# Splitting the next context early, moving late logits to a bank of their own, and one silu table load for all experts

## The chip, the cores and the metric

The kernel runs on one core of a Trainium2 chip. The metric is the device time of one execution in microseconds (us), the median over several runs. Its engines work in parallel and wait for each other by semaphores: TensorE (PE) multiplies, ScalarE (ACT) applies functions and copies, VectorE (DVE) does elementwise work and reductions, GpSimd (POOL) and SyncE (SP) mainly issue DMA transfers. SBUF is the memory that the engines share, PSUM the one into which TensorE writes, in banks of 512 float32 per partition.

## The reference

Four sequences of 1024 tokens, width 1024, float32. Three layers, each with a layernorm ahead and a residual behind:

```
x = x + attention(layernorm(x))                     # 16 heads, causal, rotary
x = x + mix(layernorm(x), ctx)                      # below
x = x + experts(layernorm(x))                       # 64 experts, 8 for each token

def mix(t, ctx):                                    # ctx [B, 1024, 512], D = 128
    query, key = ctx @ Wq.T + bq, ctx @ Wk.T + bk   # [B, 1024, 128]
    attention = softmax(query @ key.T)              # [B, 1024, 1024]
    return t @ attention.T                          # features are mixed, [B, 1024, 1024]

def experts(t):
    logits = t @ gate.T                             # 64 per token
    ...                                             # top 8, some experts mapped onto others
    y = (silu(t @ Wgate[e]) * (t @ Wup[e])) @ Wdown[e]
```

## The kernel before

Every float32 product is made from three: both operands are split into a high part (a rounded copy, made by ACT) and a low part (operand less high part, made by DVE), and `split_product` issues high x high, high x low and low x high into one PSUM bank. So each operand passes ACT, then DVE, before TensorE may use it.

The program has four stages: self attention, mixing (`mix_features`), routing, and the experts (`experts`). Each engine has its own list of instructions, written out by hand; the order within a list is fixed, and an instruction that waits holds up all behind it on that engine. TensorE's order is the schedule.

**Mixing** goes over the four batches b. For a batch the context (512 x 1024, four quarters of 256 columns, one DMA each into one of the two slots of `stage`) is split into `at_hi` and `at_lo`, which later hold the attention matrix. `project_ctx(b, n)` makes queries and keys of half n of the columns (L912) with 24 matmuls; ACT and DVE split these into `qk` (`split_qk`, `rest_of_qk`, L1055 and L1152). Then follow eight rows of blocks i: `energies` into `ps_b` (L926), `maxima` on DVE (L1161), `exps` on ACT (L1071), `invert` on DVE, `normalise_rows` on ACT (L1076), `turn_attention` (eight transposes, L939), and a split into `at_hi` and `at_lo` (L1080, L1170). While ACT and DVE do that, TensorE gets halves of the attention output's projection for token blocks 0 and 1 as filling work: `PARTS` lists them and `FILL` says after which energies each comes (L739). The projection's input is loaded into `stage`, too, and split into `split[:, 0:2]` (`split_attn_out`, L1087, `rest_of_attn_out`, L1175).

Then comes the loop over the batch's eight token blocks: `project`, layernorm (`normalise(2, g)`, L1198), `turn(2, g)` (transposes), `split_ln2` and `rest_of_ln2` (L1092, L1209), `mix` (48 matmuls into `ps_b`), `add_mix`, a second layernorm (`normalise(3, g)`), its store, `turn(3, g)`, a copy to `x3_t` (L1097), and `route_logits` (L996), the 64 logits of the experts, one block behind the mix. The last block's transposes, its logits and the two halves of the next context's projection come after the last mix, in turns. The next context can only be split after it, as `at_hi` and `at_lo` are in use until then (`split_ctx` waits for `xm_ok`, L1052).

**Experts.** A loop over 64 experts (`for_experts`, L1574): `super_block` handles 512 rows of an expert, an inner loop `tail_block` 128 more each, if there are more. At the top of each round every engine reads from SBUF how many tail blocks lie before this expert and the next (`tails_before`, L1571). Weights stream through a ring of three slots `raw_w`; ACT copies the high parts (`split`, L1883), DVE makes the low ones (`rest_of`, L2062), and TensorE's first layer of an expert waits for them. After the first two chunks and the last block's result, ACT runs one tiny silu on `warm`:

```
                finish_last(e + t0)
                act.activation(warm[:, :], warm[:, :], ACT.Silu)
                split(2)
```

ACT's functions need a table in the engine; the compiler places the ACT_TABLE_LOAD instructions, they are in no line of the kernel.

## Time and profile before

| | us |
|---|---|
| median of the three runs shown | 7848.82 (7845.66 to 7859.39) |
| the profiled execution | 7843.7 |
| its span in the profile | 7841.7 |
| TensorE busy | 7236.3 (92%) |
| DVE, ACT, POOL busy | 4006.6, 3616.8, 1745.8 |

The span is what the profile covers, from the first to the last instruction; a little lies around it. The profile's rows name an instruction by the line of the kernel, the engine, and the tile written and read. A line of a helper stands for all its callers: L908 to L910 are all split products of the mixing, L1702 to L1704 those of the experts, told apart by their tiles (`ps_r` and `xw_hi`: context projection; `ps_b` and `xattn_qk`: energies; `ps_a`: attention output's projection; `ps_b` and `at_hi`: mix). What stands in brackets behind an instruction is the idle time of its engine before it and what ended it. The granted clock is the share of full speed (2.4 GHz) at which TensorE was let run.

### The profile page before, as it was taken

Reading aid. Unit: us, or ns where it says so; the run is one execution under the profiler, and the core shown is the slowest. Engines: PE = TensorE matmul, PEld = TensorE weight load, DVE = VectorE, ACT = ScalarE, POOL = GpSimd, SP = SyncE. Lnnn points to the kernel's source line nnn. Section 1 sums busy time; section 2 is a strip of 40 time slices with the busy share of each in tenths; the row PEclk is TensorE's granted clock in tenths of the full one; section 3 lists DMA queues with packets and bytes.
Section 4 is the critical chain, followed back from the end, with each engine's and each line's share of the span. In section 5 each row is a group of like instructions: output and inputs, shape, how many; then the busy total and the mean of one; then the engine's idle time right before and its main releaser. Section 6 shows DMA issues by size and latency. Waiting matters only on the chain.

```text
span 7841.7 us, 126591 instructions
## 1 busy us (share of the span) xinstructions
PE 7236.3 (92%) x39855; PEld 6135.6 (78%) x39856; DVE 4006.6 (51%) x8015; ACT 3616.8 (46%) x6744; POOL 1745.8 (22%) x1646
## 2 busy tenths in 40 slices
PE   8997997997996889985699999999999999999999
PEld 7886886886885777874588888888888888888887
DVE  6666666666665433345444444444444444444444
ACT  5665664665665221120244444444444444444444
POOL 1111111111110000000233333333333333333333
PEclk9998998998998999997799999999999999999999
DMA  1101111111111222121356555565555565555655
GB/s 58 34 25 47 30 33 43 34 28 41 33 33 64 67 68 84 65 71 40 113 161 169 159 157 159 156 174 158 158 158 158 160 180 158 158 160 158 161 158 147
DMA packets 290687, 826.52 MB, mean 105 GB/s; under 512 B 36000, under 2 KB 111776, under 8 KB 290336
## 3 DMA queue, kind: packets, MB, share of 16 engines
q0 software_dynamic: 98928, 365.58, 20.2%
q1 hardware_dynamic: 191408, 456.61, 17.5%
q8 instruction: 178, 2.92, 0.2%
q14 instruction: 173, 1.42, 0.1%
HBM read 615.37 MB, written 206.70 MB: 105 GB/s over the span
## 4 chain that ended last, share of the span: by engine, by line
PE 48%; issue 2%; DVE 1%; ACT 1%; ACTq 1%; POOL 0%; DMA 0%; DVEq 0%; POOLq 0%
PE ps_gu L1702 10%; PE ps_gu L1704 10%; PE ps_gu L1703 10%; PE ps_y L1702 4%; PE ps_y L1704 4%; PE ps_y L1703 4%; PE ps_xe L1722 3%; PE ps_xe L1731 1%; PE ps_l L1711 1%; ACTq L1572 1%; DVE gu_lo L2062 1%; ACT gu_hi L1883 1%; PE ps_h L1814 0%; DVE logits L1976 0%; ACT xtail_hi L1855 0%
## 5 line engine op out<-in xcount | busy, mean ns | idle before, releaser
L1702 PE MATMUL ps_gu<-xs_hi,gu_hi 128*128 128x512 f32 x3072 | 1223.7, 398 | 45.7 <-DVE gu_lo L2062 45.7
L1704 PE MATMUL ps_gu<-xs_hi,gu_lo 128*128 128x512 f32 x3072 | 1205.4, 392 | 0.0
L1703 PE MATMUL ps_gu<-xs_lo,gu_hi 128*128 128x512 f32 x3072 | 1200.6, 391 | 0.0
L347 PE MATMUL ps_qkv<-w_hi,xt_hi 128*128 128x384 f32 x1920 | 709.0, 369 | 52.0 <-DVE v L637 51.9
L1702 PEld LDWEIGHTS ps_gu<-xs_hi,gu_hi 128*128 128x128 f32 x3072 | 577.9, 188 | 189.7 <-DVE gu_lo L2062 73.6
L1681 POOL TENSOR_TENSOR dn_lo<-raw_w,dn_hi 128x512 fp32r<-128x512 f32 x384 | 485.1, 1300 | 907.1 <-ACT dn_hi L1883 907.1
L1704 PEld LDWEIGHTS ps_gu<-xs_hi,gu_lo 128*128 128x128 f32 x3072 | 577.4, 188 | 129.4
L1703 PEld LDWEIGHTS ps_gu<-xs_lo,gu_hi 128*128 128x128 f32 x3072 | 578.2, 188 | 120.6
L707 DVE TENSOR_TENSOR pt_lo<-ps_t,pt_hi 128x512 fp32r<-128x512 f32 (+3 forms) x768 | 424.8, 553 | 451.9 <-ACT pt_hi L556 439.0
L347 PE MATMUL ps_qkv<-w_hi,xt_lo 128*128 128x384 f32 x1920 | 651.5, 339 | 0.0
L347 PE MATMUL ps_qkv<-w_lo,xt_hi 128*128 128x384 f32 x1920 | 649.4, 338 | 0.0
L1702 PE MATMUL ps_y<-dn_hi,hs_hi 128*128 128x512 f32 x1536 | 628.6, 409 | 0.0
L1895 ACT ACTIVATE hs_hi<-act_s 128x512 fp32r<-128x512 f32 x192 | 121.3, 632 | 1081.7 <-DVE act_s L2067 1081.7
L2062 DVE TENSOR_TENSOR gu_lo<-raw_w,gu_hi 128x512 fp32r<-128x512 f32 x768 | 482.3, 686 | 252.5 <-ACT gu_hi L1883 251.0
L1704 PE MATMUL ps_y<-dn_hi,hs_lo 128*128 128x512 f32 x1536 | 606.8, 395 | 0.0
L1703 PE MATMUL ps_y<-dn_lo,hs_hi 128*128 128x512 f32 x1536 | 606.2, 395 | 0.0
L2067 DVE TENSOR_TENSOR act_s<-ps_gu,act_s 128x512 f32<-128x512 f32 x192 | 132.7, 691 | 898.7 <-PE ps_gu L1704 898.7
L2022 DVE TENSOR_TENSOR xs_lo<-ps_xe,xs_hi 128x512 fp32r<-128x512 f32 x520 | 334.4, 685 | 478.5 <-ACT xs_hi L1847 478.5
L556 ACT ACTIVATE pt_hi<-ps_t 128x512 fp32r<-128x512 f32 (+3 forms) x768 | 375.1, 488 | 343.3 <-PE ps_t L433 328.6
L1659 POOL DMA_INDIRECT out<-y_sup,scatter_s x192 | 303.1, 1579 | 1012.1 <-ACT y_sup L1905 983.0
L1905 ACT ACTIVATE y_sup<-ps_y,w_now 128x512 f32<-128x512 f32 x384 | 264.4, 689 | 438.4 <-PE ps_y L1704 421.5
L502 ACT ACTIVATE probs<-probs,inv_sum 128x128 f32<-128x128 f32 (+7 forms) x512 | 397.6, 777 | 120.1 <-DVE inv_sum L665 114.0
(296 smaller groups left out, 16403.3 us busy)
## 6 DMA issues: line engine op xcount, KB each, us to landing
raw_w<-w_gu SPq DMA_DIRECT2D x384, 512.0 KB, 4.0
raw_w<-w_down SPq DMA_DIRECT2D x192, 512.0 KB, 6.8
w_raw<-wqkv SPq DMA_DIRECT2D x260, 192.0 KB, 2.6
out<-residual SPq DMA_DIRECT2D x36, 512.0 KB, 2.6
probs<-x SPq DMA_DIRECT2D x32, 512.0 KB, 3.8
attn_out<-out_t POOLq DMA_DIRECT2D x128, 128.0 KB, 2.2
residual<-x SPq DMA_DIRECT2D x32, 512.0 KB, 4.9
stage<-attn_out SPq DMA_DIRECT2D x32, 512.0 KB, 5.7
```

Of the source, the lines that this page charges most:

```text
L347: mm = pe.matmul(out, xs[:, k, a], ws[:, k, :], start=(n == 0), stop=(n == 3 * HB - 1))
L502: act.activation(probs[g][:, i, 0:keys], probs[g][:, i, 0:keys], ACT.Copy, scale=inv_sum[:, n:n + 1]).then_inc(norm_ok, 1)
L556: act.activation(pt_hi[:, s % 2, off:], ps_t[:, (TB - 1 + at) % 2, off:], ACT.Copy).then_inc(tile_hi_ok, 1)
L707: dve.tensor_tensor(pt_lo[:, s % 2, off:], ps_t[:, (TB - 1 + at) % 2, off:], raw(pt_hi[:, s % 2, off:]), ALU.subtract).then_inc(tile_lo_ok, 1)
L1659: pool.indirect_dma_start(out, bass.IndirectOffsetOnAxis(ap=scatter_s[:, i:i + 1], axis=0), y_sup[:, i % 2, :], None, compute_op=ALU.add). ...
L1681: pool.tensor_tensor(dn_lo[:, f, a], raw_w[:, f, a], raw(dn_hi[:, f, a]), ALU.subtract).then_inc(dn_lo_ok, 1)
L1702: pe.matmul(out, a_hi, w_hi, start=first, stop=False)
L1703: pe.matmul(out, a_hi, w_lo, start=False, stop=False)
L1704: return pe.matmul(out, a_lo, w_hi, start=False, stop=last)
L1905: act.activation(y_sup[:, i % 2, a], ps_y[:, a], ACT.Copy, scale=w_now[:, i:i + 1]).then_inc(ys_ok, 1)
L2022: dve.tensor_tensor(xs_lo[:, ks, a], ps_x1[:, c * BANK:(c + 1) * BANK].rearrange("p (k c) -> p k c", c=P), raw(xs_hi[:, ks, a]), ALU.subtr ...
L2062: dve.tensor_tensor(gu_lo[:, c // 2, b], raw_w[:, c % RING, a], raw(gu_hi[:, c // 2, b]), ALU.subtract).then_inc(lo_ok, 1)
```

## The change

In the mixing:
- The four quarters of the next context go to four places: the first to `split[:, 0:2]` (free once the batch's attention outputs are projected), the second to the second half of `qk` (free after the batch's energies), the third and fourth to `at_hi` and `at_lo` as before. `project_ctx` therefore works on quarters, 256 columns a matmul.
- SyncE loads the first two quarters two blocks earlier, the third and fourth within the last block. ACT and DVE split the first two before the last mix, the others after it.
- TensorE's order at the end of a batch: turn(2, last), mix(last, 0), turn(3, last - 1), mix(last, 1), project_ctx 0, logits of block 6 (into `ps_a`, first bank), project_ctx 1, turn(3, last). The logits of block 7 go into the second bank of `ps_a`, after the next batch's first energies and the first filling projection.
- The filling projections come at i = 0, 1, 2, 3, 5, 6, 7 instead of 1, 2, 3, 4, 6, 7 and after the loop; the attention outputs are split one or two instructions earlier, and the normalised block 0 goes into the space of `x3_t`, in DVE's round 6.

In the experts: the tiny silu moves from each round to once before the loop, and DVE's low parts of the first two chunks (`first_weights`) come before the round's reads of the block counts.

```diff
@@ -736,7 +736,7 @@
     PARTS = [(i, c, part) for i in range(2) for c in range(HALVES) for part in range(2)]
-    FILL = {1: PARTS[0], 2: PARTS[1], 3: PARTS[2], 4: PARTS[3], 6: PARTS[4], 7: PARTS[5]}
+    FILL = dict(zip((0, 1, 2, 3, 5, 6, 7), PARTS))
@@ -752,9 +752,14 @@
-ctx_hi_sb, ctx_lo_sb = at_hi[:, 0:CB, :], at_lo[:, 0:CB, :]
...
+first_x2 = x3_t[:, :, :].rearrange("p k c -> p (k c)")
+ctx_sb = [[split[:, n, :].rearrange("p (a c n) -> p a c n", a=2, n=QW) for n in range(2)],
+          [qk[:, 2 * n:2 * n + 2, BANK:].rearrange("p a (c n) -> p a c n", n=QW) for n in range(2)],
+          [t[:, 0:CB, 0:QW].rearrange("p (a c) n -> p a c n", a=2) for t in (at_hi, at_lo)],
+          [t[:, 0:CB, QW:2 * QW].rearrange("p (a c) n -> p a c n", a=2) for t in (at_hi, at_lo)]]
@@ -873,21 +877,22 @@
                 load_attn(g + 2)
-            elif b + 1 < B:
-                sp.wait_ge(ot_lo, START + g + 1)
-                load_ctx(b + 1, i + 2 - TB)
+            if i in (TB - 4, TB - 3) and b + 1 < B:
+                sp.wait_ge(ot_lo, START + g + 3)
+                load_ctx(b + 1, i + 4 - TB)
+            if i == TB - 1 and b + 1 < B:
+                rest_of_ctx(b + 1)
...
-            rest_of_ctx(b + 1)
+            first_attn(b + 1)
+        store_x3(b * TB + TB - 1)
+        if b + 1 < B:
...
-            first_attn(b + 1)
-        else:
-            store_x3(N - 1)
@@ -915,12 +920,13 @@
             pe.wait_ge(proj_lo, START + (b * 2 + n) * 2)
-            pe.wait_ge(r_read, START + max(0, b * TB - 1))
+            pe.wait_ge(r_read, START + max(0, b * TB - 2))
...
-            half_n = slice(n * BANK, (n + 1) * BANK)
-            for c in range(CB):
-                mm = split_product(ps_r[:, w, :], xw_hi[:, c, w * D:(w + 1) * D], xw_lo[:, c, w * D:(w + 1) * D],
-                                   ctx_hi_sb[:, c, half_n], ctx_lo_sb[:, c, half_n], c == 0, c == CB - 1)
+            for q in range(2):
+                hi, lo = ctx_sb[2 * n + q]
+                for c in range(CB):
+                    mm = split_product(ps_r[:, w, q * QW:(q + 1) * QW], xw_hi[:, c, w * D:(w + 1) * D], xw_lo[:, c, w * D:(w + 1) * D],
+                                       hi[:, c // 2, c % 2, :], lo[:, c // 2, c % 2, :], c == 0, c == CB - 1)
@@ -955,7 +961,8 @@
             pe.wait_ge(x1_ok, START + g)
-            pe.wait_ge(r_read, START + g // TB * TB)
+        pe.wait_ge(r_read, START + g // TB * TB - (g % TB == 0 and c == 0 and g > 0))
@@ -976,8 +983,9 @@
                 pe.wait_ge(t3_read, START + g)
+        src = first_x2 if which == 2 and i == 0 else work[:, which - 2, :]
...
-            mm = pe.transpose(ps_t2[:, k * P:(k + 1) * P], work[:, which - 2, k * P:(k + 1) * P], ident[:, :])
+            mm = pe.transpose(ps_t2[:, k * P:(k + 1) * P], src[:, k * P:(k + 1) * P], ident[:, :])
@@ -1013,29 +1022,33 @@
                 turn_attention(b, i - 1)
-        project(g + 1, 1, (0,))
+            elif b:
+                route_logits(g - 1, ps_a[:, BANK:])
         turn_attention(b, TB - 1)
...
         project(g + 1, 1, (1,))
-        for i in range(TB):
-            if i >= 1:
-                if i + 1 < TB:
-                    project(g + i + 1, 0, (0, 1))
-                turn(2, g + i)
-                if i + 1 < TB:
-                    project(g + i + 1, 1, (0, 1))
-                turn(3, g + i - 1)
+        mix(g, 0)
+        mix(g, 1)
+        for i in range(1, TB - 1):
+            project(g + i + 1, 0, (0, 1))
+            turn(2, g + i)
+            project(g + i + 1, 1, (0, 1))
+            turn(3, g + i - 1)
             mix(g + i, 0)
-            if i >= 1:
-                route_logits(g + i - 1, ps_r[:, 0, :])
+            route_logits(g + i - 1, ps_r[:, 0, :])
             mix(g + i, 1)
         last = g + TB - 1
+        turn(2, last)
+        mix(last, 0)
+        turn(3, last - 1)
+        mix(last, 1)
         if b + 1 < B:
             project_ctx(b + 1, 0)
-        turn(3, last)
+        route_logits(last - 1, ps_a[:, 0:BANK])
         if b + 1 < B:
             project_ctx(b + 1, 1)
-        route_logits(last, ps_a)
+        turn(3, last)
+    route_logits(N - 1, ps_a[:, BANK:])
@@ -1049,8 +1062,13 @@
+            act.wait_ge(wo_ok, START + b * TB)
+        elif q == 1:
+            act.wait_ge(e_ok, START + b * TB)
+        else:
...
-        act.activation(ctx_hi_sb[:, :, q * QW:(q + 1) * QW], raw_ctx(q), ACT.Copy).then_inc(ctx_hi, 1)
+        act.activation(ctx_sb[q][0], raw_ctx(q), ACT.Copy).then_inc(ctx_hi, 1)
@@ -1106,18 +1124,19 @@
         g = b * TB
+        split_attn_out(g)
         for i in range(TB):
+            if i == 4:
+                split_attn_out(g + 1)
             exps(b, i)
...
                 split_attention(b, i - 2)
-            if i == 5:
-                split_attn_out(g + 1)
+            elif i == 0 and b:
+                copy_logits(g - 1, ps_a[:, BANK:])
             normalise_rows(b, i)
-            if i == 0:
-                split_attn_out(g)
         split_attention(b, TB - 2)
         split_attention(b, TB - 1)
-        for i in range(TB):
+        for i in range(TB - 1):
             split_ln2(g + i)
@@ -1125,16 +1144,20 @@
         last = g + TB - 1
+        split_ln2(last)
         if b + 1 < B:
...
             split_ctx(b + 1, 1)
-            split_qk(b + 1, 0)
-        copy_ln3(last)
+        copy_ln3(last - 1)
         if b + 1 < B:
...
             split_ctx(b + 1, 3)
+            split_qk(b + 1, 0)
+        copy_logits(last - 1, ps_a[:, 0:BANK])
+        if b + 1 < B:
             split_qk(b + 1, 1)
-        copy_logits(last, ps_a)
+        copy_ln3(last)
+    copy_logits(N - 1, ps_a[:, BANK:])
@@ -1146,8 +1169,8 @@
         dve.wait_ge(ctx_hi, START + b * QUARTERS + q + 1)
-        a = slice(q * QW, (q + 1) * QW)
-        dve.tensor_tensor(ctx_lo_sb[:, :, a], raw_ctx(q), raw(ctx_hi_sb[:, :, a]), ALU.subtract).then_inc(ctx_lo, 1)
+        hi, lo = ctx_sb[q]
+        dve.tensor_tensor(lo, raw_ctx(q), raw(hi), ALU.subtract).then_inc(ctx_lo, 1)
@@ -1195,7 +1221,8 @@
             dve.wait_ge(x3_out, START + g * 16)
-        dve.tensor_scalar(work[:, s, :], res[:, g % 2, :], mean_var[:, s, 0:1], rstd[:, s:s + 1],
+        dst = first_x2 if which == 2 and i == 0 else work[:, s, :]
+        dve.tensor_scalar(dst, res[:, g % 2, :], mean_var[:, s, 0:1], rstd[:, s:s + 1],
@@ -1220,19 +1247,21 @@
         g = b * TB
+        rest_of_attn_out(g)
         for i in range(TB):
+            if i == 4:
+                add_projection(g)
             maxima(b, i)
+            if i == 4:
+                rest_of_attn_out(g + 1)
             if i >= 2:
...
             invert(b, i)
-            if i == 0:
-                rest_of_attn_out(g)
             if i == 5:
-                add_projection(g)
-                rest_of_attn_out(g + 1)
                 find_moments(2, g)
+            if i == 6:
+                normalise(2, g)
         rest_of_attention(b, TB - 2)
-        normalise(2, g)
         rest_of_attention(b, TB - 1)
@@ -1240,6 +1269,9 @@
                 normalise(2, g + i + 1)
+            elif b + 1 < B:
+                rest_of_ctx(b + 1, 0)
+                rest_of_ctx(b + 1, 1)
@@ -1248,14 +1280,13 @@
         if b + 1 < B:
-            rest_of_ctx(b + 1, 0)
-            rest_of_ctx(b + 1, 1)
+            rest_of_ctx(b + 1, 2)
+            rest_of_ctx(b + 1, 3)
         find_moments(3, last)
+        if b + 1 < B:
+            rest_of_qk(b + 1, 0)
         normalise(3, last)
         if b + 1 < B:
-            rest_of_qk(b + 1, 0)
-            rest_of_ctx(b + 1, 2)
-            rest_of_ctx(b + 1, 3)
             rest_of_qk(b + 1, 1)
@@ -1571,9 +1602,11 @@
-def for_experts(eng, super_block, tail_block):
+def for_experts(eng, super_block, tail_block, first=None):
...
+        if first:
+            first(e)
@@ -1864,6 +1897,7 @@
     act.wait_ge(set_up, START + 13)
+    act.activation(warm[:, :], warm[:, :], ACT.Silu)
@@ -1907,7 +1941,6 @@
         finish_last(e + t0)
-        act.activation(warm[:, :], warm[:, :], ACT.Silu)
@@ -2053,14 +2086,18 @@
+    def rest_of(e, c):
+        for q in range(2):
+            dve.wait_ge(hi_ok, START + e * 2 * CHUNKS + 2 * c + q + 1)
+            a = slice(q * BANK, (q + 1) * BANK)
+            b = slice(c % 2 * HALF + q * BANK, c % 2 * HALF + (q + 1) * BANK)
+            dve.tensor_tensor(gu_lo[:, c // 2, b], raw_w[:, c % RING, a], raw(gu_hi[:, c // 2, b]), ALU.subtract).then_inc(lo_ok, 1)
+    def first_weights(e):
+        rest_of(e, 0)
+        rest_of(e, 1)
...
-        def rest_of(c):
-            for q in range(2):
-                dve.wait_ge(hi_ok, START + e * 2 * CHUNKS + 2 * c + q + 1)
-                a = slice(q * BANK, (q + 1) * BANK)
-                b = slice(c % 2 * HALF + q * BANK, c % 2 * HALF + (q + 1) * BANK)
-                dve.tensor_tensor(gu_lo[:, c // 2, b], raw_w[:, c % RING, a], raw(gu_hi[:, c // 2, b]), ALU.subtract).then_inc(lo_ok, 1)
@@ -2144,7 +2179,7 @@
-    for_experts(dve, super_block, tail_block)
+    for_experts(dve, super_block, tail_block, first_weights)
```

The diff leaves out: the same bank and wait changes at four more places, the reshaped view of `stage`, and calls of `rest_of` that got the expert's number as an argument. Indentation is cut by eight.

## Rows read from the trace of the kernel before

**Rows 1.** Windows: us, busy time of each engine, granted clock, DMA.
```profile
3110.77:3166.60 55.83, 45.47 (x218) 35.84 (x218) 26.84 (x32) 29.39 (x36) 0.74 (x2) 0.94 0.04 10
3114.80:3123.40 8.60, 6.83 (x18) 4.90 (x19) 2.69 (x4) 4.58 (x7) 0.00 (x0) 0.60 0.21 61
3807.00:7829.00 4022.00, 3984.58 (x21562) 3311.64 (x21563) 1822.93 (x3315) 1806.78 (x3180) 1308.64 (x1021) 1.00 0.59 161
```

**Rows 2.** Timeline of TensorE, end of batch 1: start, duration, instruction, wait.
```profile
3065.44 1.03 PE L980 MATMUL ps_t<-ident,work 128*128 128x128 f32 x8
3071.46 1.71 PE L980 MATMUL ps_t<-ident,work 128*128 128x128 f32 x8 [4.99 <-DVE split L1209]
3090.62 0.50 PE L908 MATMUL ps_r<-at_hi,xw_hi 128*128 128x512 f32 x1 [3.71 <-DVE at_lo L1150]
...
3096.31 1.03 PE L980 MATMUL ps_t<-ident,work 128*128 128x128 f32 x8
3101.79 0.50 PE L908 MATMUL ps_r<-at_hi,xw_hi 128*128 128x512 f32 x1 [4.45 <-DVE at_lo L1150]
...
3109.04 1.89 PE L1000 MATMUL ps_a<-gate_sb,x_t 128*128 128x64 f32 x16
3110.77 0.50 PE L908 MATMUL ps_b<-xattn_qk 128*128 128x512 f32 x1
```

**Rows 3.** TensorE's waits in the energies of batch 2 (total, times, longest).
```profile
PE ps_a L908 <- DVE split L1175: 4.5, 2, 3.0
PE ps_b L908 <- ACT work L1071: 3.1, 2, 2.6
PE ps_t L980 <- DVE work L1198: 1.8, 1, 1.8
PE ps_t L950 <- ACT work L1076: 0.9, 1, 0.9
```

**Rows 4.** Groups by line on DVE and ACT, 3064.4 to 3166.6 us.
```profile
L1161 DVE TENSOR_REDUCE mix_small<-ps_b 128x1 f32<-128x1024 f32 x8 | 9.7, 1214 | 7.6 <-PE ps_b L910 7.6
...
L1071 ACT ACTIVATE work<-ps_b,mix_small 128x1024 f32<-128x1024 f32 x8 | 8.9, 1116 | 14.9 <-DVE mix_small L1161 14.9
```

**Rows 5.** Timeline of TensorE, matmuls of 256 columns in a tail block.
```profile
4817.24 0.28 PE L1702 MATMUL ps_gu<-gu_hi,xtail_hi 128*128 128x256 f32 x1
4817.36 0.28 PE L1703 MATMUL ps_gu<-gu_lo,xtail_hi 128*128 128x256 f32 x1
```

**Rows 6.** All table loads of the run, groups by line on ACT.
```profile
L1883 ACT ACT_TABLE_LOAD x64 | 82.1, 1283 | 58.4 <-issue 58.4
L1910 ACT ACT_TABLE_LOAD x64 | 82.1, 1283 | 1.2
L472 ACT ACT_TABLE_LOAD x1 | 1.3, 1283 | 5.9 <-PEq L69 5.9
```

**Rows 7.** Timeline around the start of an expert, all engines.
```profile
4885.40 1.28 ACT L1883 ACT_TABLE_LOAD   x1 [0.98 <-issue]
...
4886.69 2.19 ACT L1883 ACTIVATE gu_hi<-raw_w 128x512 fp32r<-128x512 f32 x4
...
4887.10 0.39 PE L1704 MATMUL ps_y<-dn_hi,hs_lo 128*128 128x512 f32 x1
4887.36 1.90 DVE L2062 TENSOR_TENSOR gu_lo<-raw_w,gu_hi 128x512 fp32r<-128x512 f32 x3 [2.11 <-ACT gu_hi L1883]
...
4888.10 0.50 PE L1702 MATMUL ps_gu<-xs_hi,gu_hi 128*128 128x512 f32 x1 [0.62 <-DVE gu_lo L2062]
...
4888.44 0.40 PE L1703 MATMUL ps_gu<-xs_lo,gu_hi 128*128 128x512 f32 x1
```

**Rows 8.** TensorE's waits in the experts.
```profile
PE ps_gu L1702 <- DVE gu_lo L2062: 45.7, 64, 8.3
```

**Rows 9.** Reads of the block counts before one expert, by queue.
```profile
L1572 PEldq SEQ_ASSERT  x2: 18/18/18, 4884.7 to 4885.4; - x2
L1572 DVEq SEQ_ASSERT  x2: 23/28/33, 4885.8 to 4887.0; - x2
```

20 lines of the change are left out of this document (10 added, 10 removed).

## The prediction, made before the changed kernel was run

> **What bounds the kernel now.** The table of stretches comes first. In the experts (3807 to 7829 us) TensorE is busy 3984.6 of 4022 us at a granted clock of 1.00, so only TensorE's own gaps can be won there. In the mixing, the loop over eight token blocks has none; the gaps sit in the stretch around the next context and in the 56 us stage of energies, where the granted clock also falls to 0.94 [rows 1]. The timeline of TensorE then shows the end of a batch: from the turn of the last block (3065.44) to the next batch's first energies (3110.77) are 45.33 us, with waits of 4.99, 3.71 and 4.45 [rows 2]. The list of waits gives 10.3 us for the energies [rows 3]. For the experts the list gives one reason, gu_lo: 45.7 us in 64 waits, one of 8.3, so (45.7 - 8.3) / 63 = 0.59 each [rows 8]. Ends of matmuls are modelled, 0.39 us after the start, while the next one can start 0.24 later (24 of them in 5.69 us, 3090.62 to 3096.31) [rows 2, 7], so each wait costs 0.16 us more than its row says, and the first matmul after it delays the next by 0.34 instead of 0.24 (4888.10 to 4888.44), 0.10 more [rows 7].
>
> **Context and logits (mixing), between batches 1 and 2.** The change loads the first two quarters of the next context two blocks earlier and splits them, into other buffers, while DVE waits for the last mix. Their four instructions stay; they move off the path.
> - Removed: the wait before the first half's projection, 3.71 + 0.16 = 3.87 us. mix(last, 1) now ends and project_ctx(0) starts.
> - Removed: the wait before the second half, from 3096.31 + 0.79 (eight transposes) to 3101.79 = 4.69 us [rows 2]. Its splits can start at the end of the last mix, and take add_mix, two ACT and two DVE instructions, about 3.7 us in all for tiles of this size at 1.1 to 1.2 us with DVE and ACT overlapping [rows 4]; over them lie project_ctx(0) (5.7 us) and the moved logits (1.7). The covers are worth 3.7 us if they fail.
> - Removed with it: the low clock behind that wait. The second projection took 3101.79 to 3109.04 = 7.25 us, the first 3090.62 to 3096.31 = 5.69: 1.56 us.
> - Moved: the last block's logits, 3109.04 to 3110.77 = 1.73 us, to behind the next first energies [rows 2]. It is paid again below.
> - Added: one wait before the energies, since turn(3) (0.79 us) no longer covers the split of the second projection on ACT and DVE. Before, the energies started 1.73 us after the projection, as soon as the logits let them [rows 2], and the chain itself needs about 1.75; without the logits 0.96 us stay open.
> - Added: each half is now 48 matmuls of 256 columns instead of 24 of 512. Starts of such ones are 0.12 us apart (48 in 5.7 us to be expected) against 0.24 [rows 5]: +0.45 us a batch, with 0.1 for the first half's tiles being split just before the second half may start.
> - The wait of 4.99 stays: DVE still normalises block 6 before it splits block 7's transposes.
> Sum: 3.87 + 4.69 + 1.56 + 1.73 - 0.96 - 0.55 = 10.3 us.
>
> The 256 columns are the place where a page would speak against the change. The row: 256-column matmuls, each with weights of its own, start 0.12 us apart [rows 5], so loads are hidden. The Trainium skill, "TensorE: Matmul & The Clock Gate", section "LDWEIGHTS (loading the stationary operand)", gives 128 columns / 1.2 = 107 ns a load, and its section on packing says that loads overlap only other row groups; an estimate from it is 0.21 us for each pair and 9 us more a batch, some 37 in all. The trace disagrees.
>
> **The energies.** I walk the new order with 1.45 us for six matmuls, 2.8 for a half projection, 0.79 for transposes, and 1.21 and 1.12 us for maxima and exps, normalising about like exps [rows 4]. From the first energies (0): ACT copies block 7's transposes and splits the attention output, DVE its rest, so the projection starts at 2.85 instead of 1.45 (wait 1.4); logits to 7.35; energies 1 at 7.35, 3 at 17.45, 4 at 22.5. Block 4 now has no projection: turning 3 waits 1.3, and energies 5, behind add_projection, maxima and a longer ACT queue, 1.65. Energies 7 wait 1.1 for DVE's moments. The last projection stands before turn 6, so turn 7 waits 4.2 for maxima, exps and normalising of block 7, and the turn of the normalised block 1.4 for rest_of_attention(6). That is 11.05 us; the same six waits of before are 10.3 + 6 x 0.16 = 11.3 [rows 3]. So: 55.83 - 11.3 + 11.05 + 1.73 (logits) = 57.3. Before, 8.6 us of this stage ran at 0.60 [rows 1], which cost about 0.4 x 6.8 busy us = 2.7. Nothing says where a dip falls in the new order: none gives 54.6, one as before 57.3. I take half, 56.0: no gain, -1.4 to +1.4 a batch.
>
> Batch 0 has no logits there and its first attention tile is long split when the energies start: about 3.0 us less, 0.4 back for the narrower matmuls. At the very end the logits of block 30 move behind the last mix, into the wait for the last normalised block: 1.7 us. SyncE's new waits hold up no store: in DVE's order each stands before the add_mix whose result that store needs.
>
> Mixing: 3 x (10.3 - 0.1) + 2.6 + 1.7 = 35 us.
>
> **The experts.** Every expert begins with an ACT_TABLE_LOAD of 1.28 us in front of a plain copy, and has another for the silu warm-up; the whole of attention and mixing, whose exps also stand in loops, has one [rows 6]. The chain at the start of an expert: table load 4885.40, first split at 4886.69 (0.64 us), its rest on DVE 4887.36, TensorE 4888.10, while the last matmul had started at 4887.10 and could have been followed at 4887.34 [rows 7]. Two edits act here. With silu loaded once before the loop, state at entry and at the loop's end agree, and both loads should vanish: split at 4885.40, done 4886.04. DVE's reads of the block counts end only at 4887.0 [rows 9]; alone they would still make its rest late by 0.5 us. The new order puts the first splits ahead of them: rest from 4886.07 to 4886.76, 0.57 us before TensorE needs it. TensorE's own reads end at 4885.4, under queued matmuls [rows 9]. What comes later on DVE (w_now, gather indices) is about 1.1 us later against TensorE; its users are the gathers for the next turns, which stand whole layers behind. Gain per expert 0.59 + 0.16 + 0.10 = 0.86 us, the first about the same by the reads; 64 x 0.86 = 55 us. If a load stays at the top, the gain is 0.
>
> The trace shows that copies run behind the silu load without a load of their own, but one stands ahead of the first copy of each round [rows 6, 7]. The Trainium skill, "ScalarE: Activation LUTs", section "Table sets: the hidden batching unit", says that copy is in every set; by that rule no load in the loop is needed, and the one at the top is only the compiler's. The trace agrees as to the copies behind silu. The page's other figure, 2.66 us a switch with its drain, no row shows: the next activation starts 0.01 us behind the 1.28.
>
> **Rivals.**
> 1. The load at the loop's top stays. For it: it is there 64 times. Against: one load in all earlier loops [rows 6]. The experts gain nothing: 7759 + 55 = 7814 us.
> 2. The second half of the context comes late after all (its transfers start behind the last block's store and x load) and a wait of 4.6 us comes back three times: 7759 + 14 = 7773. Against it: they can start about 12 us before the last mix ends.
> 3. Narrow matmuls cost their shown 0.28 us each [rows 5]: 4 x 96 x (0.28 - 0.12) = 61: 7820. Against it: the starts in the same rows. The page's rule on weight loads would act here too, with less.
> 4. Slower: TensorE without gaps gets a lower clock in the experts. Seen there: 1.00 [rows 1]. At the energies' 0.94 it would cost 4022 x (1/0.94 - 1) = 257: 8016 us. It decides from a clock of 0.974 down. Against it: gaps lowered the clock so far, not their absence.
>
> **Numbers.** 35 + 55 = 90 us off. The profiled execution took 7843.7 (span 7841.7, 2.0 around it), 5.1 below the median of the runs shown, 7848.8; I take 90 from the median: 7759 us; the new profile's span should be about 7752. Chances: forecast 0.80, rival 1 0.09, rival 2 0.07, rival 3 0.02, rival 4 0.01, nothing at all (two of them together) 0.01. The forecast's own range, with dips (4 x 1.4), gaps (0.1 us an expert either way) and the spread of the medians, is 7742 to 7776; with rival 2 to 7788. A change of 0.2% (16 us) is about what the measurement can tell: faster 0.97, same 0.02, slower 0.01.
>
> **What would show it.** In the changed kernel: one or two table loads on ACT in all; no TensorE wait for gu_lo from the second expert on, a stage of some 3967 us at clock 1.00; no wait before ps_r's projections or one under 0.3 us; first energies 35 us behind the turn of block 7; waits of 1.4 and 4.2 us in the energies, which should last 54.6 to 57.3 us. Wrong: loads left in the loop, a wait for the context, or the energies beyond 58 us.

## The result, and the profile after

The changed kernel takes 7749.9 us (median of 4 runs, 7742.4 to 7753.8) where the kernel before takes 7850.9 (4 runs beside them, 7845.7 to 7859.4): a ratio of 0.9868, 95% interval 0.9856 to 0.9881, or 101 us less. The forecast was 7759 in a range of 7742 to 7776, or to 7788 with rival 2. The runs of the two kernels don't overlap. The profiled execution has a span of 7747.5 us (7841.7 before).

First the windows of the changed kernel: energies of batch 1, its eight blocks up to the turn of the last one, the stretch from there to the next energies, and the experts. Columns: stretch, us, then busy time (instructions) of TensorE, its weight loads, VectorE, ACT and POOL, granted clock, DMA share, GB/s.

```profile
2833.44:2887.47 54.03, 47.09 (x232) 38.59 (x233) 26.82 (x32) 29.67 (x37) 0.74 (x2) 0.94 0.04 10
2887.47:3052.52 165.05, 165.05 (x817) 137.79 (x816) 60.06 (x77) 19.46 (x24) 9.59 (x26) 1.00 0.24 80
3052.52:3086.81 34.29, 28.70 (x186) 25.79 (x184) 15.51 (x19) 9.58 (x12) 1.48 (x4) 0.95 0.48 154
3764.22:7734.68 3970.46, 3970.38 (x21562) 3316.61 (x21563) 1834.51 (x3315) 1630.92 (x2991) 1298.71 (x1021) 1.00 0.60 163
```

They answer to [rows 1]. In the experts TensorE is now busy in all but 0.1 us of its stretch. Taken from the starts of the same instructions in both timelines, in us:

| stretch | before | after | won | forecast |
|---|---|---|---|---|
| energies of batch 0 | 55.8 | 51.4 | 4.4 | 2.6 with the first context |
| energies of batches 1, 2, 3 | 55.8, 55.9, 55.9 | 54.0, 53.2, 53.2 | 7.1 | -0.3 |
| turn of the last block to the next energies, three times | 45.4, 45.3, 45.3 | 34.8, 34.3, 34.3 | 32.6 | 30.9 |
| turn of the last block to the last logits copied, batch 3 | 32.5 | 31.3 | 1.2 | 1.7 |
| first expert matmul to the last one | 4022.3 | 3970.5 | 51.8 | 54 |
| last logits copied to first expert matmul | 176.4 | 175.3 | 1.1 | 0.9 |
| from the start to the first context matmul | 2561.0 | 2564.8 | -3.9 | 0 |

The rows add up to 94.3, the difference of the two spans (94.2). The last one is code that the change doesn't touch; the experiments show that it varies by itself. So does the mixing stage, by up to 10.9 us between profiled executions of the same mixing code (below), so the gains of the mixing in this table are those of one execution each.

The end of batch 0 on TensorE (start, duration, instruction, wait ahead of it and who ended it):

```profile
2798.61 1.04 PE L988 MATMUL ps_t<-ident,work 128*128 128x128 f32 x8
2804.54 0.79 PE L913 MATMUL ps_b<-at_hi,split 128*128 128x512 f32 x1 [4.89 <-DVE split L1236]
...
2806.41 0.63 PE L914 MATMUL ps_b<-at_lo,split 128*128 128x512 f32 x1
2806.84 0.63 PE L915 MATMUL ps_b<-at_hi,split 128*128 128x512 f32 x1
...
2818.66 0.28 PE L913 MATMUL ps_r<-split,xw_hi 128*128 128x256 f32 x1
...
2824.26 1.89 PE L1009 MATMUL ps_a<-gate_sb,x_t 128*128 128x64 f32 x16
2826.03 0.36 PE L913 MATMUL ps_r<-at_hi,xw_hi 128*128 128x256 f32 x1
...
2831.71 1.03 PE L988 MATMUL ps_t<-ident,work 128*128 128x128 f32 x8
2833.44 0.50 PE L913 MATMUL ps_b<-xattn_qk 128*128 128x512 f32 x1 [0.69 <-DVE xattn_qk L1179]
```

Against [rows 2]: both waits before ps_r's projections are gone and both projections run at full clock (5.60 and 5.68 us); one wait of 0.69 is new; the wait of 4.9 for the last block's split has stayed. Behind it the mix matmuls start 0.43 us apart, not 0.23: the low clock is part of that wait's price.

TensorE's waits in the experts and all table loads of the run, against [rows 8] and [rows 6]:

```profile
PE ps_gu L1735 <- DVE gu_lo L2094: 7.3, 1, 7.3
```

```profile
L472 ACT ACT_TABLE_LOAD x1 | 1.3, 1283 | 5.9 <-PEq L69 5.9
L1900 ACT ACT_TABLE_LOAD x1 | 1.3, 1283 | 29.5 <-PEq L69 29.5
```

And the start of one expert, against [rows 7]: no table load, the rest of chunk 0 on VectorE 0.7 us behind ACT, and TensorE goes from ps_y to ps_gu in 0.23 us.

```profile
4829.27 2.20 ACT L1917 ACTIVATE gu_hi<-raw_w 128x512 fp32r<-128x512 f32 x4 [1.00 <-issue]
...
4829.94 2.49 DVE L2094 TENSOR_TENSOR gu_lo<-raw_w,gu_hi 128x512 fp32r<-128x512 f32 x4 [0.83 <-ACT gu_hi L1917]
...
4830.95 0.40 PE L1737 MATMUL ps_y<-dn_hi,hs_lo 128*128 128x512 f32 x1
4831.18 0.39 PE L1735 MATMUL ps_gu<-xs_hi,gu_hi 128*128 128x512 f32 x1
```

The waits of TensorE in the energies of batch 1, against [rows 3]. Each row is a total, the number of waits and the longest; the walk had 1.4 where the first projection's 1.0 stands, 1.3 for turn 3 and 4.2 for turn 7 where ps_r's 4.3 stands for both, 1.65 for energies 5 (the row of 1.3) and 1.1 for energies 7, 1.4 for the turn of the normalised block (ps_t). The 0.7 is the new wait ahead of the first energies. The rows leave out the 0.16 us behind each wait.

```profile
PE ps_r L956 <- ACT work L1094: 4.3, 2, 3.4
PE ps_b L913 <- ACT work L1089: 1.3, 1, 1.3
PE ps_a L913 <- DVE split L1198: 1.0, 1, 1.0
PE ps_b L913 <- DVE xattn_qk L1179: 0.7, 1, 0.7
PE ps_t L988 <- DVE at_lo L1193: 0.3, 1, 0.3
```

### The profile page after: what moved, and what is told of

Same layout as the page of the kernel before. It is cut to its first block, busy times and chain, and to the rows that moved or that the text cites. A ratio compares the mean times of both kernels' runs of the same rounds, so it can differ in the third digit from the quotient of the medians.

```text
span 7747.5 us, 126837 instructions
## 1 busy us (share of the span) xinstructions
PE 7219.9 (93%) x40047; PEld 6153.2 (79%) x40048; DVE 4017.3 (52%) x8015; ACT 3437.1 (44%) x6554; POOL 1735.5 (22%) x1646
## 4 chain that ended last, share of the span: by engine, by line
PE 51%; DVE 0%; DMA 0%; POOL 0%; issue 0%; ACT 0%; DVEq 0%; POOLq 0%; ACTq 0%
PE ps_gu L1737 10%; PE ps_gu L1735 10%; PE ps_gu L1736 10%; PE ps_y L1735 5%; PE ps_y L1737 5%; PE ps_y L1736 5%; PE ps_xe L1755 3%; PE ps_xe L1764 1%; PE ps_l L1744 1%; PE ps_h L1847 0%; DVE logits L2009 0%; DMA out<-y_sup,scatter_s 0%; DMA x_rows<-rows,gather_s 0%; DVE xs_lo L2055 0%; DVE at_hi L2002 0%
## 5 line engine op out<-in xcount | busy, mean ns | idle before, releaser
L347 PE MATMUL ps_qkv<-w_hi,xt_hi 128*128 128x384 f32 x1920 | 709.5, 370 | 51.9 <-DVE v L637 51.8
L1917 ACT ACTIVATE gu_hi<-raw_w 128x512 fp32r<-128x512 f32 x768 | 427.2, 620 | 230.4 <-DMA raw_w<-w_gu 170.8
```

Source lines behind the costliest of these rows:

```text
L347: mm = pe.matmul(out, xs[:, k, a], ws[:, k, :], start=(n == 0), stop=(n == 3 * HB - 1))
L1917: act.activation(dst[:, a], raw_w[:, c % RING, a], ACT.Copy).then_inc(hi_ok, 1)
```

## The experiments

"Mixing stage" below is the time from the first context matmul to the start of the last logits: 1065.45 us before, 1020.17 after. Ratios are to the kernel before on the same chip.

**The two parts, each alone.** The one kernel has the mixing of before and the experts of after, the other the reverse; no line besides.

> The mixing of before with the experts of after (silu loaded once ahead of the loop, VectorE's first_weights ahead of its reads). Theory: the two parts of the change add up, so this one is worth what the stage of the experts showed in the trace of after, 53 us (52 to 55): a ratio of 0.9933, first expert matmul to last ps_y start 3970.5 us (4022.3 before), boundary of the mixing 45.3 us as before. Rival: part of those 53 us comes from the mixing's new state (a higher clock or other DMA traffic carried over), then the stage stays over 3980 us here.

> The mixing of after with the experts of before. Theory: the mixing stage alone gives its 45 us (mixing stage 1024.1 us against 1069.4; ratio 0.9943), and the experts stay at 4022 us with 64 table loads ahead of the first copy and 64 for the silu. Rival: the stage before it also moved by 3.9 us between the two traces although its code is the same; if the change causes that, this kernel shows it too, with its first context matmul at 2564.8 and not at 2561.0.

Experts alone: 7796.1 us, ratio 0.9925 (0.9908 to 0.9941), stage of the experts 3969.9. Mixing alone: 7796.3 us, ratio 0.9929 (0.9912 to 0.9945), mixing stage 1022.9, experts 4023.2 with 64 and 64 table loads. (The 1024.1 and 1069.4 of its expectation are counted to the copy of the last logits, 3.9 us later.) The parts add up: 4022.3 - 3969.9 = 52.4 and 1065.5 - 1022.9 = 42.5 make 94.9, against 51.8 + 45.3 = 97.1 for both together. (By the medians the parts are 56.0 and 55.9 us, 112 against 101 for both; the intervals of the ratios, about 13 us either way for each part, allow for that.) The rival of a carried-over state falls: the stage of the experts is 3969.9 us with the mixing of before. The first context matmul started at 2561.1 with the changed mixing and at 2568.3 with the old one; over all kernels here it lay between 2558.8 and 2569.1, with the same code ahead of it. So the 3.9 us in the table are variation of that stage, not the change.

One thing was not expected: with the mixing's code as before, the kernel with the new experts needed 1073.1 us for that stage, 7.7 more than before. The granted clock accounts for it. Take the busy time of TensorE in windows of 1 us, times the share of the clock that it lacks there, and add this up over the mixing stage (us, one profiled execution each; the last rows belong to experiments below):

| kernel | mixing | stage | low clock | stage less low clock |
|---|---|---|---|---|
| before | before | 1065.5 | 25.4 | 1040.0 |
| e_silu_once_only | before | 1066.8 | 26.6 | 1040.2 |
| e_experts_only | before | 1073.1 | 33.7 | 1039.4 |
| e_dve_first_only | before | 1076.3 | 36.9 | 1039.4 |
| after | after | 1020.2 | 19.4 | 1000.8 |
| m_mixing_only | after | 1022.9 | 21.8 | 1001.1 |
| m_late_loads | later loads | 1020.9 | 20.1 | 1000.8 |
| m_logits_early | earlier logits | 1024.0 | 24.1 | 999.9 |
| m_fill_late | later filling | 1019.5 | 14.9 | 1004.6 |
| m_keep_warm | dummies | 1020.9 | 17.3 | 1003.7 |
| v_rest_first | VectorE's order | 1011.0 | 20.1 | 990.9 |
| v_split_first | more order | 1001.3 | 14.5 | 986.7 |
| v_order_all | more order | 991.9 | 10.4 | 981.5 |

Four executions of one mixing code differ by 10.9 us in the stage and by 0.8 once the low clock is taken out. Of the 45.3 us that the change won in the mixing, 39.2 are in the last column and 6.0 in the low clock, and the second part could have come out some us either way. The split is not exact between different orders: low clock that a later wait covers costs nothing and is taken out all the same (see the dummy matmuls). One such stretch in e_experts_only (a wait on TensorE, then a window: stretch, us, busy, clock, DMA share, GB/s): it begins 1.3 us behind the end of a wait of 2.96, where the profiled execution of before has the same wait (3148.21) and keeps its clock.

```profile
3156.49 0.50 PE L908 MATMUL ps_a<-wo_hi,split 128*128 128x512 f32 x1 [2.96 <-DVE split L1175]
```

```profile
3157.00:3162.00 5.00, 5.00 (x20) 0.66 0.00 0
```

**The experts' two edits, each alone.** Both on the kernel before.

```diff
+            act.activation(warm[:, :], warm[:, :], ACT.Silu)     # e_silu_once_only: ahead of the loop
...
-                act.activation(warm[:, :], warm[:, :], ACT.Silu)
```

```diff
-            for_experts(dve, super_block, tail_block)                # e_dve_first_only
+            for_experts(dve, super_block, tail_block, first_weights)
```

> Before, with one edit: the silu warm-up stands once ahead of the loop; VectorE still reads its block counts ahead of the rest of chunk 0. Theory: the table loads vanish from the loop and ACT's first split is done at about 4886.04 on before's clock, but VectorE is busy with its reads to 4887.0, so TensorE starts at about 4887.75 in place of 4888.10: 0.35 us an expert, 22 us in all, ratio 0.9972, and a wait for gu_lo of some 0.25 us stays in every round. Rival: the reads aren't in the way and all 53 us come here (0.9933).

> Before, with the other edit alone: VectorE's rest of chunks 0 and 1 ahead of its reads of the block counts; the silu warm-up stays in each round, with both table loads. Theory: ACT's table load and first split end at 4887.33 on before's clock and VectorE's reads at 4887.0, so TensorE is held by ACT: 0 to 2 us in all, ratio 1.000. Rival: the reads are what holds TensorE, and this edit gives 20 us or more by itself (0.9975 or less).

Silu once: 7837.9 us (10 runs), ratio 0.9983 (0.9974 to 0.9993), experts 4009.9: 12.4 us won. VectorE's order alone: 7852.9 us (10 runs), ratio 1.000 (0.999 to 1.0009), experts 4022.0. The edits are a pair: 12.4 and 0.3 us in the stage apart, 52.4 together, since two things end the same wait. (By the medians Silu once wins 14 us and VectorE's order nothing.) Silu once, waits in the experts and the start of an expert:

```profile
PE ps_gu L1702 <- DVE gu_lo L2062: 31.6, 63, 8.3
```

```profile
4886.16 0.68 DVE L2022 TENSOR_TENSOR xs_lo<-ps_xe,xs_hi 128x512 fp32r<-128x512 f32 x1
...
4887.01 2.19 ACT L1884 ACTIVATE gu_hi<-raw_w 128x512 fp32r<-128x512 f32 x4 [1.00 <-issue]
...
4888.69 0.39 PE L1704 MATMUL ps_y<-dn_hi,hs_lo 128*128 128x512 f32 x1
4888.81 2.50 DVE L2062 TENSOR_TENSOR gu_lo<-raw_w,gu_hi 128x512 fp32r<-128x512 f32 x4 [1.97 <-ACT gu_hi L1884]
...
4889.55 0.50 PE L1702 MATMUL ps_gu<-xs_hi,gu_hi 128*128 128x512 f32 x1 [0.47 <-DVE gu_lo L2062]
```

No table load stands ahead of ACT's split, and its first part is long done when VectorE starts at 4888.81, 1.97 us behind the end of its last instruction (4886.84). The row names ACT, but ACT isn't what held it: with the reads behind the rest, the same idle time is 0.83 in after's expert shown above. What fills the gap are the reads of the block counts on VectorE's queue (count, shortest, median and longest in ns, start of the first and the last):

```profile
L1572 DVEq TENSOR_LOAD <-starts x2: 316/556/796, 4886.9 to 4887.6; - x2
L1572 DVEq SEQ_ASSERT  x2: 23/28/33, 4887.4 to 4888.6; - x2
```

They begin as VectorE's last instruction ends, and the last part of them stands 0.2 us before the next one. So two register reads on VectorE cost 1.97 us here from instruction to instruction. The 22 us expected were worked out with the end of the reads' own rows, 1.75 us [rows 7, 9], and were 0.15 us an expert too many (0.19 measured for 0.35); the waits that stay are (31.6 - 8.3) / 62 = 0.38 us for 0.25.

In the other kernel the load is still there and ends the wait, as in [rows 7]:

```profile
4896.07 1.28 ACT L1885 ACT_TABLE_LOAD   x1 [0.98 <-issue]
4897.37 2.19 ACT L1885 ACTIVATE gu_hi<-raw_w 128x512 fp32r<-128x512 f32 x4
...
4898.78 0.50 PE L1704 MATMUL ps_gu<-xs_hi,gu_hi 128*128 128x512 f32 x1 [0.61 <-DVE gu_lo L2063]
```

**Are the early loads of the context needed?** After, with the two loads at the place of before.

```diff
-                    if i in (TB - 4, TB - 3) and b + 1 < B:
-                        sp.wait_ge(ot_lo, START + g + 3)
-                        load_ctx(b + 1, i + 4 - TB)
+                    if i in (TB - 2, TB - 1) and b + 1 < B:
+                        sp.wait_ge(ot_lo, START + g + 1)
+                        load_ctx(b + 1, i + 2 - TB)
```

> After, with the loads of the next context's first two quarters issued two blocks later, as before did. Theory: the early loads are not needed; the first quarter is split behind the last block's transposes and the second one arrives before project_ctx(0) is due, so the boundary stays at 34.3 us and the time at after's (ratio to before 0.987). Rival: the second quarter comes behind the store and the x load of its block and late; a wait before project_ctx(0) of 2 to 4 us comes back three times, 6 to 12 us in all, boundary 36.5 to 38.5.

7748.6 us, ratio 0.9865 (0.9849 to 0.9882), mixing stage 1020.9: no difference. ACT now waits for the second quarter's transfer, but in the cover of the last mix:

```profile
3068.70 1.06 ACT L1071 ACTIVATE xattn_qk<-stage 128x1024 fp32r<-128x1024 f32 x1 [8.24 <-DMA stage<-ctx_t]
```

The projection starts at 3076.89. With 1.2 us for VectorE's part, about 6 us of slack are left. The rival's wait did not come, and it is not the time of the loads that wins at this place. What is left is the buffers of their own, which let the splits run beside the last mix; the splits without them weren't tried, since they would overwrite what the last mix reads.

**Narrow matmuls.** After, with each mix matmul as two of 256 columns.

```diff
-                n = slice(c * BANK, (c + 1) * BANK)
-                for k in range(TB):
...
+                for q in range(2):
+                    n = slice(c * BANK + q * QW, c * BANK + (q + 1) * QW)
+                    for k in range(TB):
```

> After, with every mix matmul of 512 columns issued as two of 256 with a weight load each: 32 blocks x 48 = 1536 become 3072. Theory: weight loads are hidden under matmuls of 256 columns, starts are 0.12 us apart and two of them take what one of 512 takes (0.237): 1536 x 0.003 = 5 us and the change of tiles nothing; ratio to before 0.987 to 0.989. Rival (page rule on weight loads): the load of 128 columns isn't covered, each pair costs 0.19 to 0.21 us more, 290 to 320 us in all, ratio about 1.025.

7760.1 us, ratio 0.9881 (0.9864 to 0.9897), mixing stage 1040.8, 20.6 us more (11.5 and 14.7 against the medians of m_late_loads and m_fill_late on the same chip; in the profiled execution 9 us of it are missing again in stages that the edit doesn't touch). The weight loads are hidden; the rival's 290 to 320 us are not there.

```profile
2911.32 0.28 PE L913 MATMUL ps_b<-at_hi,split 128*128 128x256 f32 x1
2911.44 0.28 PE L914 MATMUL ps_b<-at_lo,split 128*128 128x256 f32 x1
2911.56 0.28 PE L915 MATMUL ps_b<-at_hi,split 128*128 128x256 f32 x1
```

The theory's 5 us were too few: it took 0.237 us for the wide matmul, from the context projection, where those of the mix start 0.227 apart (2795.65 to 2798.37 in 12 steps, in the timeline of after). Two narrow ones take 0.24, so a pair costs 0.013 more, 20 us for 1536.

**Where the last filling stands.** After, with its seventh half projection ahead of turn 7 and not of turn 6.

```diff
-    FILL = dict(zip((0, 1, 2, 3, 5, 6, 7), PARTS))
+    FILL = dict(zip((0, 1, 2, 3, 5, 6), PARTS))
...
+                project(g + 1, 1, (0,))
                 turn_attention(b, TB - 1)
```

> After, with its seventh filling half projection (2.8 us on TensorE) moved from ahead of turn 6 to ahead of turn 7. Theory: turn 7 is bound by the chain of maxima, exps, reciprocal and normalising of block 7, which doesn't move, so the wait of 3.4 ahead of turn 7 shrinks by 2.8 to about 0.6, 2.8 us less stand ahead of turn 6, and the stage of energies stays at 53.2 to 54.0 us. Rival A: the filling is only worth its place where it is, and the stage grows by 1 to 3 us. Rival B: turn 6 comes earlier and with it the rest of its chain, and the stage shrinks by 1 us or more.

7745.4 us, ratio 0.9864 (0.9847 to 0.988), energies of batches 1 to 3 53.6, 52.7, 52.7: 0.5 us less each. The theory missed that turn 6 would have to wait: the 3.4 became 1.8 ahead of turn 6 and 1.4 ahead of turn 7, not 0.6. Turn 7 itself runs at full clock, and the turn of the normalised block waits 1.2 in place of 0.3. But that turn starts 49.90 us behind batch 1's first energies, 49.86 in after. So the theory's main point holds: a chain over ACT and VectorE sets the end of this stage, and the fillings only cover it.

**Block 7's logits ahead of the energies again.**

```diff
                 turn(3, last)
-            route_logits(N - 1, ps_a[:, BANK:])
+                route_logits(last, ps_a[:, BANK:])
```

(and the copy on ACT behind copy_ln3(last); the calls behind energies 0 go.)

> After, with block 7's logits ahead of the next batch's first energies again, behind turn(3, 7). Theory (the prediction's terms: 1.73 us moved, 0.96 of it paid back as a wait): the logits need the copy of block 7's transposes, which ACT makes behind the split of the second projection, so the first energies start 2.3 us later than in after (boundary 36.6 us), and the energies lose the 1.73 us of logits but keep the wait for the attention output they covered: the stage falls by 1.5; 0.8 us a batch more in all, 2 to 3 us in the kernel. Rival: the logits behind the energies were cover that is missed more than that, or the low clock of the energies' start comes back, 2 us a batch or more.  The other rival: their place is worth nothing.

7749.5 us, ratio 0.9869 (0.9852 to 0.9885), mixing stage 1024.0: 3.8 us more in the profile, nothing in the median. From one batch's mix to the next energies it is 1.7, 2.8 and 2.2 us longer, the energies are 0.9, 1.5 and 0.1 shorter; in batches 1 and 3 a stretch of low clock is back just behind the first energies (2830 to 2835 us and 3339 to 3343 us). The table above puts all of it down to the low clock: 24.1 us for 19.4, while the rest of the stage is 0.9 us shorter. So the 0.8 us a batch that the theory expected do not show apart from it. Whether the logits' place brings the low clock back isn't shown either, since after's own mixing code varied by 2.4 us of it between two executions (m_mixing_only).

**Dummy matmuls in the longest wait.**

```diff
+                pe.wait_ge(eexp_ok, START + (b + 1) * TB)
+                for k in range(12):
+                    pe.matmul(ps_b[:, 0:BANK], wo_hi[:, 0, 0:P], wo_hi[:, 0, 0:BANK], start=True, stop=True)
                 turn_attention(b, TB - 1)
```

> After, with twelve matmuls of 512 columns that nothing uses (2.8 us) put into the wait of 3.4 us ahead of turn 7, in a bank that is free then. Theory: the stretch of low clock that follows this wait comes from the idle time in it; TensorE's clock stays at 1.00 there, the eight transposes of turn 7 take 1.03 us in place of 1.97, and the stage of energies shrinks by 1.0 to 1.5 us (2.7 in batch 0), 5 to 7 us in the kernel. Rival A: the low clock comes from what ran before (the waits of the whole stage) or from elsewhere and stays: gain 0. Rival B: the stage only gets the dip at another place.

7742.8 us, ratio 0.986 (0.9843 to 0.9876). Turn 7 in after, and here:

```profile
2881.04 1.97 PE L956 MATMUL ps_r<-ident,work 128*128 128x128 f32 x8 [3.41 <-ACT work L1094]
```

```profile
2870.55 2.99 PE L1029 MATMUL ps_b<-wo_hi 128*128 128x512 f32 x12
2873.72 1.09 PE L956 MATMUL ps_r<-ident,work 128*128 128x128 f32 x8 [0.17 <-ACT work L1097]
```

The next instruction, the turn of the normalised block, in after and here:

```profile
2883.30 1.54 PE L988 MATMUL ps_t<-ident,x_t 128*128 128x128 f32 x8 [0.29 <-DVE at_lo L1193]
```

```profile
2875.97 1.07 PE L988 MATMUL ps_t<-ident,x_t 128*128 128x128 f32 x8 [1.17 <-DVE at_lo L1196]
```

The low clock is gone from turn 7, in all four batches, and in m_fill_late too, so it hung on the long wait there. But turn 7's transposes got 0.88 us faster and the wait behind them 0.88 longer: the turn of the normalised block needs VectorE's rest of block 6 and comes when that is done. Most of what the low clock cost at turn 7 was covered. The energies change by -1.7, -0.8, +0.4 and -0.5 us; in batch 2 a stretch of low clock has come at energies 5 (the window below). The other stretches grow by 0.7, 0.7, 0.2 and 1.8, with longer low clock behind the wait of 4.9, and the mixing stage is 1020.9 us, no shorter.

```profile
3106.00:3110.00 4.00, 2.92 (x7) 0.60 0.00 0
```

Rival B holds in part: some of the low clock moved, and some of it had cost nothing. The profiled execution is 8 us shorter than after's, but 6 of them lie ahead of the first context matmul, in the stage that varies.

**Three versions that go further.** The first takes the wait of 4.9 apart: VectorE's moments and normalising of block 6 stand in front of the split that TensorE waits for.

```diff
                     add_mix(g + i)
+                    if i == TB - 2:
+                        rest_of_ln2(g + i + 1)
                     if i < TB - 1:
                         find_moments(3, g + i)
```

> After, with one more edit on VectorE: the rest of block 7's transposes (rest_of_ln2(last)) stands ahead of the moments and the normalising of block 6. Theory: the wait of 4.9 us ahead of the last mix holds VectorE's moments and normalising of block 6, about 2.6 us; it falls to 2.3 us and turn(3, 6), which stands behind the first half of the last mix, is still covered: 4 x 2.6 = 10 us less than after, boundary 31.7 us, ratio to before 0.9855. Rival: block 6's normalising comes late instead and turn(3, 6) gets a wait of the same size, gain 0.

7738.9 us, ratio 0.985 (0.9834 to 0.9867), mixing stage 1011.0. The wait:

```profile
2803.41 0.50 PE L913 MATMUL ps_b<-at_hi,split 128*128 128x512 f32 x1 [2.44 <-DVE split L1236]
```

The blocks and what follows them got shorter by 4.7, 2.5, 4.1 and 2.4 us (in batches 0 and 2 the low clock behind the wait went too), the energies longer by 1.5, 0.7, 0.9 and 1.9, again with the low clock in them; with 0.6 less ahead of the first energies that is 9.2 us in all, for the 10 expected. The rival's wait ahead of turn(3, 6) did not come.

The second and the third also take the chain of the energies apart. v_split_first has this besides:

```diff
+                    if i == TB - 1:
+                        split_attention(b, i - 2)
                     exps(b, i)
-                    if i >= 2:
+                    if 2 <= i < TB - 1:
                         split_attention(b, i - 2)
...
                     maxima(b, i)
+                    if i == 7:
+                        normalise(2, g)
...
-                    if i == 6:
-                        normalise(2, g)
```

and v_order_all has the split ahead of the exps in every slot, and

```diff
-                    if i == 4:
-                        add_projection(g)
                     maxima(b, i)
+                    if i == 4:
+                        add_projection(g)
```

> v_rest_first, with two more moves in the energies of block 7: ACT splits block 5's turned attention ahead of the exps of block 7 (it waited behind them), and VectorE normalises the next block 0 behind the maxima of block 7, not ahead of them. Theory: turn 7 is bound by the chain over ACT and VectorE, where VectorE's reciprocal stands behind the rest of block 5 for 2.1 us; ACT's chain (normalise 6, split 5, exps 7, normalise 7) then ends at about 2879.3 on after's clock in place of 2881.0: 1.7 us less ahead of turn 7 and in the stage, 4 x 1.7 = 7 us less than v_rest_first, ratio to before about 0.984. Rival: something else of like length is bound (maxima 7, the rest of block 6), gain under 0.5 us a batch.

> v_split_first, with ACT's split of the turned attention ahead of the exps in every slot from the third on (v_split_first did it in the last one alone), and VectorE's maxima of block 4 ahead of adding the projection. Theory: in the slots with a filling half projection nothing changes, TensorE covers the chain; in slot 4, which has none, the wait of 0.93 us ahead of turn 3 goes and the exps of block 4 end at about 2849.1 in place of 2850.0 on v_split_first's clock, so energies 5 start 0.9 us earlier: 4 us less in all, mixing stage about 997.5 us against 1001.3, ratio to before 0.984. Rival: the exps come later in the slots where ACT is full (slot 4 and 5, with the split of the attention output), and the stage stays or grows.

v_split_first: 7728.1 us, ratio 0.9843 (0.9826 to 0.9859), mixing stage 1001.3. v_order_all: 7715.9 us (5 runs, 7715.3 to 7717.7), ratio 0.9829 (0.9816 to 0.9843), mixing stage 991.9. Batch 1's energies in v_order_all, as window and as waits:

```profile
2821.43:2870.66 49.23, 44.41 (x233) 36.43 (x234) 26.89 (x32) 29.54 (x37) 0.74 (x2) 1.00 0.04 11
```

```profile
PE ps_b L913 <- ACT work L1089: 1.9, 2, 1.7
PE ps_t L988 <- DVE at_lo L1193: 1.2, 1, 1.2
PE ps_a L913 <- DVE split L1198: 1.0, 1, 1.0
PE ps_r L956 <- ACT work L1094: 0.8, 1, 0.8
PE ps_b L913 <- DVE xattn_qk L1179: 0.7, 1, 0.7
```

Turn 7 waits 0.8 us in place of after's 3.4, turn 3 not at all, and the stage runs at a clock of 1.00 from end to end: 49.2 us. Each step gave more than expected (9.7 for 7, 9.4 for 4). The low clock fell by 5.6 and 4.2 us in them; it had no place in either theory. In the last step a batch from the second on wins 3.1 us in its energies: 1.4 in waits (turn 3's 0.93 gone, turn 7's 1.53 to 0.76, and 1.34 to 1.68 ahead of energies 5) and 1.6 by the low clock. After, v_rest_first and v_split_first have a stretch or two of low clock in every energies from batch 1 on; v_order_all has none there, and one each in the blocks of batches 0 to 2 (2793 to 2797, 3039 to 3043 and 3285 to 3289 us). That fewer waits are why the clock holds in the energies is what these kernels suggest, not what they isolate.

## Why the prediction was right, point by point

- **Experts, 55 us: right.** Measured 52.9 (51.8 in the stage, 0.82 an expert for 0.86, and 1.1 ahead of it), in the profile and, with 52.4 in the stage, alone in e_experts_only. Both table loads left the loop, as the step on the state at entry and at the loop's end had it; that this state is the compiler's reason was argued, and no run varies it by itself. That the second edit is needed as well is shown: 12.4 us without it. The rule of the Trainium skill, "ScalarE: Activation LUTs", section "Table sets: the hidden batching unit", that a copy is in every set, agrees with this trace: all 64 rounds of copies run with no load of their own.
- **Rival 1 (load stays), rival 3 (narrow matmuls cost 0.28) and rival 4 (lower clock without gaps): not so.** Two loads in the run; 48 narrow matmuls in 5.60 and 5.68 us against 24 wide in 5.69; the experts' clock is 1.00 with TensorE busy throughout. The estimate of 9 us a batch from the Trainium skill, "TensorE: Matmul & The Clock Gate", section "LDWEIGHTS (loading the stationary operand)", is contradicted by these rows and by m_narrow_mix.
- **The end of a batch, 10.3 us each: right.** Measured 10.5, 11.0 and 11.0. Both waits went, the low clock behind the second with them, the new wait is 0.69 + 0.16 = 0.85 for 0.96 and the narrow matmuls cost nothing for 0.55: those two terms are 0.7 us too many, the difference in batches 1 and 2 (in batch 0 the low clock behind the wait of 4.9 lasted longer and took 0.5 back). Rival 2 (the second half late) didn't come; even two blocks later the loads of the first half leave about 6 us of slack.
- **The energies: the term that was mis-sized.** The walk gave 54.6 us without low clock and 57.3 with as much as before; 56.0 was taken, and 53.2 to 54.0 are measured. In batch 2 the six waits it foresaw come to 7.2, with 0.16 us behind each 8.1, for 11.05. Of these 2.9 us, 0.9 are no fault of the waits: at full clock the turn of the normalised block waits 1.17 + 0.16, as walked (m_keep_warm, m_fill_late), and in after the slow transposes of turn 7 run in that time. So the walk counted a wait and a low clock that partly cover each other. The other 2.0 are its chains: turn 7 at 4.2 for 3.6, energies 7 at 1.1 for 0.4, 0.1 to 0.3 at the others. It set each instruction of ACT and VectorE behind the end of the last one in its row, while the next starts up to 0.1 us earlier; how much of the 2.0 that explains was not taken apart.
- **The low clock in them: a guess.** It took 2.6 before, 2.9 in batch 1 of after (half at energies 5, half at turn 7) and 1.4 and 1.5 in batches 2 and 3; the forecast put it at half of 2.7. With 11.3 - 8.1 = 3.2 for the waits, 2.6 - 1.4 = 1.2 for the clock and -1.73 for the logits, batches 2 and 3 should win 2.7; they win 2.7 and 2.6. In batch 1 the waits are 7.7 and the clock is 0.3 worse, which makes 1.6; it wins 1.8. In batch 0, which has no logits there, 4.4 are won for 3.0. With the same mixing code in m_mixing_only, low clock took 3.0, 3.0 and 1.5, and batches 1 to 3 won 4.9 in place of 7.1: that the sum came out above the forecast here is in part the luck of one execution.
- **The sum.** 90 us forecast, 94.2 in the spans. Mixing gave 10.4 more than its 35 (7.4 in the energies of batches 1 to 3, 1.7 at the ends of batches, 1.8 in batch 0, -0.5 at the end), the experts 2 less, and the untouched stage ahead took 3.9 back by its own variation. So the nearness of the sum is in part errors that cancel. By the medians 101 us went, 11 more than forecast, from a base 2 us above the one it was taken from.

## What to carry to other kernels

When two things end the same wait, price the edits as a pair: one alone gave 12 us, the other nothing, both 52. The profile names the releaser that came last by its records; register reads ahead of the waiting instruction can hold it longer, and they show only in the gap to the instruction before. Put on each in-order engine first what TensorE waits for next: such moves gave 28 us more in the mixing stage, without a new buffer (9 us less low clock among them). Before filling a wait, or pricing the low clock behind it, look at the next wait: if a chain on other engines sets it, what is won ahead of it is lost there. And when two profiles are compared, take the low clock out of both.

## What the runs showed of the hardware that was not expected

- TensorE's clock fell from its upper to its lower level (2.4 to 1.2 GHz; granted clocks down to 0.5 in windows of 1 us) at least once a batch in the mixing, in every kernel here. The stretches looked at came during or just behind waits, but not behind every wait: behind one of 2.96 us it fell in e_experts_only (0.66 over 3157 to 3162 us) and stayed up in before. It makes the same mixing code vary by 10.9 us between executions (1065.5 to 1076.3), and by 0.8 with the low clock taken out. What decides where such a stretch falls stays open.
- Two register reads on VectorE cost 1.97 us, measured from instruction to instruction where nothing covers them, 0.2 more than to the end of their own rows (e_silu_once_only). TensorE does not wait for its own, which lie under queued matmuls [rows 9].
- Matmuls of 512 columns start 0.227 us apart in the mix and 0.233 in the projections, with the same shapes (the 0.237 used above, 24 in 5.69 us, contains a first one behind a wait, whose successor starts 0.33 us later). Nothing here explains that.
